# The projection of queries and keys issued ahead of mask and scores on TensorE in 40 slots of a two-branch transformer block

## The chip, the cores and the metric

The kernel runs on one core of one Trainium2 chip. The metric is the device time of one execution in microseconds (us); less is better. All data is float32 (the mask alone is bfloat16).

## The reference

The input x is (4, 1024, 128). After a layer norm two branches read it, and their outputs are added to x: `_L0_attn_ref`, a retention block (16 heads of 8, channel group norms, a small feed-forward part with silu), and `_L0_ffn_ref`, two layers of local attention with a gated feed-forward part. The change lies in the second branch:

```
def _layer(x, wqkv, qs, ksc, wo, lg, lb, w1, b1, w2, b2):
    h = shift_token(x)
    q, k, v = jnp.split(h @ wqkv, 3, axis=-1)      # 8 heads of 64 each
    q = l2norm(q) * qs
    k = l2norm(k) * ksc
    q, k = rotary_xpos(q, k)
    o = local_attention(q, k, v)                   # windows of 64, the own and the one before
    x = x + o @ wo
    h = layernorm(shift_token(x)) * lg + lb
    a, g = jnp.split(h @ w1 + b1, 2, axis=-1)
    return x + (a * gelu(g)) @ w2 + b2
```

## The kernel before

The work goes in steps. A step (l, t) is 128 rows of all four batches in layer l (0 or 1), t from 0 to 7. Every engine runs one list of instructions, written out by hand, in 18 bodies; the engines meet only by semaphores. A body has four slots, k = 0 to 3, one for each batch. In slot k the step `new` projects batch k, the step `old` is finished for batch k, and at slot 0 the step `ff` goes through the feed-forward part. In layer 0 the retention branch of the step follows behind slot 3 (`pe_retention` and its likes on the other engines); in layer 1, for t of 2 and more, slots 1 and 2 hold the small feed-forward part of the retention branch (`block_ffn`).

The attention of one batch is a pipeline over slots. `turned` is the batch projected two slots before: its normalized queries and keys (qkn) are transposed into pT (L1006, then ScalarE copies kT and qT), and its mask (L1025) and scores (L1038) go into pS. `weighted` is the batch projected three slots before: its exponentiated scores pr are transposed into pT (L1049), ScalarE copies them to prT (L540), and they are multiplied with the values into pS (L1064). At the same time batch k of `old` has its output transposed (L1075), copied to oT by ScalarE (L594), multiplied by wo (L1081) and added to the residual by VectorE (xr, L749).

The projection of batch k is two parts on TensorE: the values into bank pV (L1099), and queries and keys into the two banks of pQK (L1133, two matmuls of 128x512). What follows on pQK: ScalarE squares it (sq, L556), VectorE sums the squares (ss, L707), then divides the weighted output (rec and o, L737 and L739), then makes the two products with the rotary tables (m1 and m2, L717, in the rows `m`), each of which adds 1 to `mul_done`. GpSimd makes the norm, the sum and the product qkn from them (L358, L360, L373, L380).

There is one pQK. So L1133 waits until both products of the batch before it are done:

```
need(eng, S["mul_done"], 2 * n)
```

VectorE's order in a slot is: maximum and subtraction of the scores of `turned` (mx L727, pr L729), the residual xr (L749), ss (L707), rec and o, the two products (L717). ScalarE's order is: kT and qT, copies of values and of the shifted input, prT (L540), oT (L594; in slot 0 with a feed-forward part hnT, L545, stands there instead, and then exp, the loading of the gelu table and gelu, L601), sq (L556), exp (L587).

Of the kernel before, what the change touches and what calls it, by code (L numbers as in the profile page):

```python
# [13 lines left out]
NB = 4  # L14
# [72 lines left out]
def need(eng, sem, value):  # L87

    if isinstance(value, int) and value <= 0:
        return  # L90
    eng.wait_ge(sem, value)


def program(nc, a, out):
    with ExitStack() as ctx:
        def sb(name, shape, dt=F32):
            return ctx.enter_context(nc.sbuf_tensor(name, shape, dt))

        def sem(name):
            return ctx.enter_context(nc.semaphore(name))  # L100
# [21 lines left out]
        wqkv = sb("wqkv", [P, DEPTH, 3 * INNER])  # L122
# [35 lines left out]
        hT = sb("hT", [P, NB, P])  # L158
# [54 lines left out]
        pQK = ctx.enter_context(nc.psum_tensor("pQK", [P, 1024], F32))  # L213
# [11 lines left out]
        def score_bank(b):  # L225
# [13 lines left out]
        LS = {n: sem(n) for n in (  # L239
            "carried", "v_kept", "h_ready", "qk_mm", "v_mm", "sq_done", "ss_done", "mul_done", "max_ss", "rn_done", "add_done",  # L240
            "qkn_done", "t_mm", "t_ev", "v_ev", "s_mm", "mx_done", "sub_done", "exp_done",
            "pt_mm", "pt_ev", "o_mm", "rec_done", "o_done", "ot_mm", "ot_ev", "wo_mm", "xr_carried", "xr_done", "hs",
            "ln_mm", "ln_bst", "ln_st", "ln_eps", "ln_rs", "hn_done", "hnt_mm", "hnt_ev", "ag_mm", "gelu_done",
            "hf_done", "w2_mm", "x2_done")}
# [27 lines left out]
        def step_count(step):  # L272

            return NT * step[0] + step[1]

        def count(step, b):
            return NB * step_count(step) + b
# [8 lines left out]
        def at(new, old, k):  # L286

            step = new if k >= 0 else old
            return (step, k % NB, count(step, k % NB)) if step else None
# [708 lines left out]
        def pe_turn(eng, b, n):  # L998

            S = LS  # L1000
            eng.wait_ge(S["qkn_done"], n + 1)
            need(eng, S["t_ev"], 2 * n)
            need(eng, S["pt_ev"], n - 1)
            for half in (1, 0):
                for j in range(4 * half, 4 * half + 4):
                    mm = eng.transpose(pT[:, j * P:(j + 1) * P], qkn[:, b % 2, j * P:(j + 1) * P], ident)  # L1006
                mm.then_inc(S["t_mm"], 1)
# [34 lines left out]
        def pe_turn_weights(eng, b, n, turned):  # L1042
            S = LS
            eng.wait_ge(S["exp_done"], n + 1)
            need(eng, S["pt_ev"], n)
            if turned:
                eng.wait_ge(S["t_ev"], 2 * (n + 2))
            for j in range(8):
                mm = eng.transpose(pT[:, j * P:(j + 1) * P], pr[:, b % 2, j, :], ident)  # L1049
            mm.then_inc(S["pt_mm"], 1)  # L1050
# [18 lines left out]
        def pe_turn_output(eng, n, bank=pM):  # L1069

            S = LS
            eng.wait_ge(S["o_done"], n + 1)
            need(eng, S["xr_done"], n)
            for j in range(4):
                mm = eng.transpose(bank[:, j * P:(j + 1) * P], o[:, j * P:(j + 1) * P], ident)  # L1075
            mm.then_inc(S["ot_mm"], 1)

        def pe_wo(eng, l, n, bank=pM):
            eng.wait_ge(LS["ot_ev"], n + 1)
            for j in range(4):  # L1080
                mm = eng.matmul(bank[:, 0:P], wo[:, l, j, :], oT[:, j, :], start=(j == 0), stop=(j == 3))  # L1081
            mm.then_inc(LS["wo_mm"], 1)

        def pe_slot(eng, new, old, ff, k):
            S = LS
            block_ffn = ff and ff[0] == 1
            turned = at(new, old, k - 2)
            weighted = at(new, old, k - 3)
            if turned:
                pe_turn(eng, turned[1], turned[2])  # L1090
            if k == 0 and old and old[0] == 0:
                pe_retention_out(eng, old[1])
            if new:
                l, n = new[0], count(new, k)
                eng.wait_ge(S["h_ready"], 2 * n + 2)
                need(eng, S["v_ev"], 2 * n)
                if k == 1 and old:
                    eng.wait_ge(S["xr_done"], count(old, 0) + 1)
                eng.matmul(pV[:, :], hT[:, k, :], wqkv[:, l, 1024:1536], start=True, stop=True).then_inc(S["v_mm"], 1)  # L1099
            if k == 1 and block_ffn:  # L1100

                need(eng, S["mul_done"], 2 * n if new else 0)
                eng.wait_ge(G["xa"], 4 * ff[1] + 4)
                for j in range(2):
                    eng.matmul(pQK[:, j * 512:(j + 1) * 512], aT[:, 4 + j, :], xa[:, :, :], start=True,
                               stop=True).then_inc(G["w1_mm"], 1)
            if turned:
                pe_scores(eng, *turned)
            if weighted:
                pe_turn_weights(eng, weighted[1], weighted[2], turned)  # L1110
            if k == 0 and ff:

                ct = step_count(ff)
                eng.wait_ge(S["hn_done"], NB * ct + NB)
                for b in range(NB):
                    mm = eng.transpose(pM[:, b * P:(b + 1) * P], hn[:, b, :], ident)
                mm.then_inc(S["hnt_mm"], 1)
            if k > 0 and old:
                if k == 1 and ff:
                    eng.wait_ge(S["x2_done"], step_count(ff) + 1)  # L1120
                if k == 2 and block_ffn:
                    eng.wait_ge(G["att"], ff[1] + 1)
                if k == 3 and block_ffn:
                    eng.wait_ge(G["osb"], ff[1] + 1)
                pe_turn_output(eng, count(old, k))
            if k == NB - 1 and new and new[0] == 0:
                pe_retention_project(eng, new[1], 0)
            if new:
                need(eng, S["mul_done"], 2 * n)
                if k == 1 and block_ffn:  # L1130
                    eng.wait_ge(G["silu"], 2 * ff[1] + 2)
                for g in range(2):
                    mm = eng.matmul(pQK[:, g * 512:(g + 1) * 512], hT[:, k, :], wqkv[:, l, g * 512:(g + 1) * 512],  # L1133
                                    start=True, stop=True)
                mm.then_inc(S["qk_mm"], 1)
            if k == 0:
                if ff:
                    pe_hidden(eng, ff, (0, 1), turned, weighted)
                if old:
                    if new:  # L1140
                        eng.wait_ge(S["v_ev"], 2 * n + 2)
                    pe_turn_output(eng, count(old, 0), pV)
                if ff:
                    pe_hidden(eng, ff, (2,), turned, weighted)
                    pe_ffn_out(eng, ff, lambda: weighted and pe_values(eng, weighted[1], weighted[2], turned))
            if k > 0 and old:
                pe_wo(eng, old[0], count(old, k))
            if weighted and not (k == 0 and ff):
                pe_values(eng, weighted[1], weighted[2], turned)
            if k == 0 and old:  # L1150
                pe_wo(eng, old[0], count(old, 0), pV)
            if k == 1 and block_ffn:
                eng.wait_ge(G["silu"], 2 * ff[1] + 2)
                eng.wait_ge(S["x2_done"], NT + ff[1] + 1)
                if old:
                    eng.wait_ge(S["xr_done"], count(old, 1) + 1)
                for j in range(2):
                    mm = eng.matmul(pM[:, :], aT[:, 6 + j, :], afh[:, j, :], start=(j == 0), stop=(j == 1))
                mm.then_inc(G["w2_mm"], 1)
            if k == 2 and block_ffn:  # L1160

                eng.wait_ge(G["fin"], ff[1] + 1)
                if old:
                    eng.wait_ge(S["xr_done"], count(old, 2) + 1)
                for b in range(NB):
                    mm = eng.transpose(pM[:, b * P:(b + 1) * P], fin[:, b, :], ident)
                mm.then_inc(G["fin_mm"], 1)
            if k == NB - 1 and old and not (new and new[0] == 0):
                pe_ln(eng, old)
# [130 lines left out]
        def pe_retention_out(eng, t):  # L1300
            eng.wait_ge(A["yt"], t + 1)
            eng.matmul(pS[:, 0:512], aT[:, 3, :], ayT[:, :], start=True, stop=True).then_inc(A["ow_mm"], 1)
# [85 lines left out]
```

## Time and profile before

| What | Value |
|---|---|
| Median of 3 runs | 1004.31 us (1003.1 to 1006.28) |
| Profiled execution | 1006.43 us, of which its span is 1004.6 us |
| TensorE busy | 871.2 us, 87% of the span |
| VectorE busy | 703.5 us, 70% |
| ScalarE busy | 660.7 us, 66% |
| GpSimd busy | 623.5 us, 62% |

The span is what the trace covers, from the first instruction to the last; the time is some 2 us more. A busy share counts an engine's own instructions, and each engine waits for others in between. PE is TensorE (PEld its weight loads), DVE VectorE, ACT ScalarE, POOL GpSimd. A float32 matmul stands in the trace as two records, so the two matmuls of L1133 are "x4".

### The profile page before, as it was taken

The numbers are of one execution on the slowest core, as the hardware profiler recorded it, in microseconds if no ns is written. First come the engines' busy times: TensorE is split into PE (matmuls) and PEld (weight loads), VectorE is DVE, ScalarE is ACT, GpSimd is POOL, SyncE is SP. The second block draws the span as 40 slices with busy tenths as digits, with TensorE's granted clock in tenths as the row PEclk, the third lists the DMA queues.
The fourth block names the chain that finished last, engine by engine and source line by source line (L and its number), as shares of the span: only waits on it lengthen the run. The fifth ranks groups of instructions, "written<-read, shape, count | busy, mean of one in ns | idle before, by whom it ended". The sixth has DMA issues, their size and how long they took to land. (4 is left out here: it accounts for less than half of the span.)

```text
span 1004.6 us, 26321 instructions
## 1 busy us (share of the span) xinstructions
PE 871.2 (87%) x10836; PEld 586.7 (58%) x10836; DVE 703.5 (70%) x1161; ACT 660.7 (66%) x1291; POOL 623.5 (62%) x491
## 2 busy tenths in 40 slices
PE   1677889989899898998989879999999999999876
PEld 1345666766567666676666556565656565656552
DVE  5865766666666667676676766969696969696843
ACT  0444775857758477674785667877786868686633
POOL 4486677675776657666576646757575757575600
PEclk9969999999999899999999989999999999999997
DMA  9100000000000000000000000000000000000000
GB/s 292 21 1 3 1 2 2 2 3 2 2 3 1 3 1 2 3 2 3 2 1 3 2 1 2 1 2 22 2 22 2 22 1 23 2 22 2 22 23 10
DMA packets 20481, 13.47 MB, mean 13 GB/s; under 512 B 4578, under 2 KB 19596, under 8 KB 20236
## 3 DMA queue, kind: packets, MB, share of 16 engines
q1 hardware_dynamic: 15108, 10.49, 3.5%
q10 hardware_dynamic: 5256, 1.31, 0.7%
q8 instruction: 87, 1.43, 0.6%
q14 instruction: 30, 0.25, 0.1%
HBM read 9.70 MB, written 2.10 MB: 12 GB/s over the span
## 5 line engine op out<-in xcount | busy, mean ns | idle before, releaser
L360 POOL TENSOR_TENSOR rn<-rn,half_neg 128x16 f32<-128x16 f32 x64 | 187.6, 2931 | 5.3
L373 POOL TENSOR_TENSOR m<-m 128x1024 f32<-128x1024 f32 x64 | 151.1, 2360 | 0.1
L358 POOL TENSOR_SCALAR rn<-ss 128x16 f32<-128x16 f32 x64 | 16.4, 256 | 199.6 <-DVE ss L707 198.4
L380 POOL TENSOR_TENSOR qkn<-m,rn 128x1024 f32<-128x1024 f32 x64 | 123.8, 1934 | 5.0
L727 DVE TENSOR_REDUCE mx<-pS 128x8 f32<-128x1024 f32 x64 | 78.0, 1219 | 68.7 <-PE pS L1038 68.7
L1133 PE MATMUL pQK<-wqkv,hT 128*128 128x512 f32 x256 | 123.9, 607 | 2.3 <-DVE m L717 2.3
L516 ACT ACTIVATE kT<-pT 128x512 f32<-128x512 f32 x64 | 38.1, 595 | 94.6 <-PE pT L1006 94.1
L556 ACT ACTIVATE sq<-pQK 128x1024 f32<-128x1024 f32 x64 | 65.4, 1022 | 26.4 <-PE pQK L1133 26.3
L707 DVE TENSOR_REDUCE ss<-sq 128x16 f32<-128x1024 f32 x64 | 77.5, 1211 | 6.1 <-ACT sq L556 6.1
L729 DVE TENSOR_TENSOR pr<-pS,mx 128x1024 f32<-128x1024 f32 x64 | 78.4, 1225 | 2.2
L540 ACT ACTIVATE prT<-pT 128x1024 f32<-128x1024 f32 x64 | 65.0, 1016 | 17.4 <-PE pT L1049 16.5
L1064 PEld LDWEIGHTS pS<-vmix,prT 128*64 128x64 f32 x1024 | 64.5, 137 | 20.3 <-issue 15.3
L717 DVE TENSOR_TENSOR m<-pQK,rope 128x1024 f32<-128x1024 f32 x64 | 75.6, 1215 | 0.0
L717 DVE TENSOR_TENSOR m<-pQK,tab 128x1024 f32<-128x1024 f32 x64 | 75.4, 1210 | 0.0
L1006 PE MATMUL pT<-cst,qkn 128*128 128x128 f32 x512 | 70.5, 282 | 5.2 <-POOL qkn L380 4.9
L1064 PE MATMUL pS<-vmix,prT 128*64 128x65 f32 x1024 | 73.2, 225 | 2.1 <-DVE pr L729 2.1
L587 ACT ACTIVATE pr<-pr 128x1024 f32<-128x1024 f32 x64 | 67.6, 1056 | 10.1 <-DVE pr L729 9.1
L1064 PE MATMUL pS<-vown,prT 128*64 128x65 f32 x1024 | 73.3, 225 | 0.0
L1099 PE MATMUL pV<-wqkv,hT 128*128 128x512 f32 x128 | 69.6, 627 | 4.1 <-DVE xr L749 2.1
L1049 PE MATMUL pT<-cst,pr 128*128 128x128 f32 x512 | 69.9, 279 | 0.0
L1192 PE MATMUL pT<-hnT,w 128*128 128x512 f32 (+1 forms) x128 | 62.7, 613 | 6.5 <-DVE hidden L813 5.0
L1038 PE MATMUL pS<-kT,qT 64*64 64x128 f32 x2048 | 68.1, 271 | 0.0
(168 smaller groups left out, 2038.5 us busy)
## 6 DMA issues: line engine op xcount, KB each, us to landing
x<-in_L_attn_x SPq DMA_DIRECT2D x4, 512.0 KB, 9.1
xs<-in_L_attn_x SPq DMA_DIRECT2D x8, 256.0 KB, 2.9
out<-aqkT SPq DMA_DIRECT2D x8, 256.0 KB, 2.2
wqkv<-in_L_ffn_wqkv SPq DMA_DIRECT2D x2, 768.0 KB, 9.9
tab<-in_k_tab SPq DMA_DIRECT2D x1, 1024.0 KB, 10.4
w<-in_L_ffn_w SPq DMA_DIRECT2D x2, 341.0 KB, 10.5
wo<-in_L_ffn_wo SPq DMA_DIRECT2D x2, 256.0 KB
cst<-in_k_cst ACTq DMA_DIRECT2D x1, 404.5 KB, 3.8
```

The lines of the kernel that those rows point to most:

```text
L360: eng.tensor_tensor(rn[:, k % 2, :], rn[:, k % 2, :], half_neg[:, 0:2 * H], ALU.pow).then_inc(S["rn_done"], 1)
L373: eng.tensor_tensor(m1[:, k % 2, :], m1[:, k % 2, :], m2[:, k % 2, :], ALU.add).then_inc(S["add_done"], 1)
L380: eng.tensor_tensor(qkn[:, k % 2, :].rearrange("p (h d) -> p h d", d=DH), m1[:, k % 2, :].rearrange("p (h d) -> p h d", d=DH), rn[:, k % 2 ...
L707: eng.tensor_reduce(ss[:, k % 2, :], sq[:, :].rearrange("p (h d) -> p h d", d=DH), AX.X, ALU.add).then_inc(S["ss_done"], 1)
L717: eng.tensor_tensor(m[:, k % 2, :].rearrange(shape, g=2, h=H, **sizes), src, by, ALU.mult).then_inc(S["mul_done"], 1)
L727: eng.tensor_reduce(mx[:, :], sc, AX.X, ALU.max).then_inc(S["mx_done"], 1)
L729: eng.tensor_tensor(pr[:, b % 2, :, :], sc, mx[:, :].unsqueeze(2).broadcast_to([P, H, P]), ALU.subtract).then_inc(S["sub_done"], 1)
L1006: mm = eng.transpose(pT[:, j * P:(j + 1) * P], qkn[:, b % 2, j * P:(j + 1) * P], ident)
L1049: mm = eng.transpose(pT[:, j * P:(j + 1) * P], pr[:, b % 2, j, :], ident)
L1064: mm = eng.matmul(pS[64 * w:64 * w + 64, col0:col0 + DH + 1], prT[:, i, 64 * w:64 * w + 64], (vown if w else vmix)[b][:, 2 * j + g, :], st ...
L1099: eng.matmul(pV[:, :], hT[:, k, :], wqkv[:, l, 1024:1536], start=True, stop=True).then_inc(S["v_mm"], 1)
L1133: mm = eng.matmul(pQK[:, g * 512:(g + 1) * 512], hT[:, k, :], wqkv[:, l, g * 512:(g + 1) * 512], start=True, stop=True)
```

## The change

In the slots where `new` and `turned` exist, k is 0, 1 or 2, and k = 1 isn't shared with `block_ffn` (which puts its own product into pQK in that slot), the two matmuls into pQK and their wait for `mul_done` are issued directly behind the values' matmul into pV, ahead of mask and scores. In the other slots they stay where they were. No instruction is added or removed. The slots are: slot 2 of step (0,0); slots 0 to 2 of the steps (0,1) to (0,7), (1,0) and (1,1); slots 0 and 2 of (1,2) to (1,7). These are 1 + 27 + 12 = 40 of 64.

```diff
+        def pe_queries_keys(eng, step, k):
+
+            n = count(step, k)
+            need(eng, LS["mul_done"], 2 * n)
+            for g in range(2):
+                mm = eng.matmul(pQK[:, g * 512:(g + 1) * 512], hT[:, k, :], wqkv[:, step[0], g * 512:(g + 1) * 512],
+                                start=True, stop=True)
+            mm.then_inc(LS["qk_mm"], 1)
+
...
                     eng.matmul(pQK[:, j * 512:(j + 1) * 512], aT[:, 4 + j, :], xa[:, :, :], start=True,
                                stop=True).then_inc(G["w1_mm"], 1)
+            early = new and turned and k < NB - 1 and not (k == 1 and block_ffn)
+            if early:
+                pe_queries_keys(eng, new, k)
             if turned:
                 pe_scores(eng, *turned)
...
-            if new:
-                need(eng, S["mul_done"], 2 * n)
+            if new and not early:
                 if k == 1 and block_ffn:
                     eng.wait_ge(G["silu"], 2 * ff[1] + 2)
-                for g in range(2):
-                    mm = eng.matmul(pQK[:, g * 512:(g + 1) * 512], hT[:, k, :], wqkv[:, l, g * 512:(g + 1) * 512],
-                                    start=True, stop=True)
-                mm.then_inc(S["qk_mm"], 1)
+                pe_queries_keys(eng, new, k)
```

The order on TensorE in a slot 1 of layer 0, before:

```order
L1006 MATMUL pT<-cst,qkn 128x128 x8
L1099 MATMUL pV<-wqkv,hT 128x512
L1025 MATMUL pS<-mask 64x512 x4
L1038 MATMUL pS<-kT,qT 64x128 x16
L1049 MATMUL pT<-cst,pr 128x128 x8
L1075 MATMUL pM<-cst,o 128x128 x4
L1133 MATMUL pQK<-wqkv,hT 128x512 x2
L1081 MATMUL pM<-oT,wo 128x128 x4
```

and with the change:

```order
L1006 MATMUL pT<-cst,qkn 128x128 x8
L1108 MATMUL pV<-wqkv,hT 128x512
L1089 MATMUL pQK<-wqkv,hT 128x512 x2
L1025 MATMUL pS<-mask 64x512 x4
L1038 MATMUL pS<-kT,qT 64x128 x16
L1049 MATMUL pT<-cst,pr 128x128 x8
L1075 MATMUL pM<-cst,o 128x128 x4
L1081 MATMUL pM<-oT,wo 128x128 x4
```

The pair into pQK has moved ahead of mask, scores and both transposes, and the product with wo now follows the transposes directly. Line numbers behind the new function are 8 or 9 higher.

The order on TensorE in slot 0 of a step of layer 0 with a feed-forward part, before:

```order
L1099 MATMUL pV<-wqkv,hT 128x512
L1025 MATMUL pS<-mask 64x512 x4
L1038 MATMUL pS<-kT,qT 64x128 x16
L1049 MATMUL pT<-cst,pr 128x128 x8
L1116 MATMUL pM<-cst,hn 128x128 x4
L1133 MATMUL pQK<-wqkv,hT 128x512 x2
L1192 MATMUL pT<-hnT,w 128x512 x2
```

and with the change:

```order
L1108 MATMUL pV<-wqkv,hT 128x512
L1089 MATMUL pQK<-wqkv,hT 128x512 x2
L1025 MATMUL pS<-mask 64x512 x4
L1038 MATMUL pS<-kT,qT 64x128 x16
L1049 MATMUL pT<-cst,pr 128x128 x8
L1128 MATMUL pM<-cst,hn 128x128 x4
L1200 MATMUL pT<-hnT,w 128x512 x2
```

Here the pair stood between the transposes of hn and the first matmul on hnT; now nothing does. The lists of VectorE, ScalarE, GpSimd and the queues are the same as before.

## Rows read from the trace of the kernel before

**Rows 1.** The page, shares of the span in the chain that ended last.

```profile
PE 20%; DVE 18%; ACT 7%; issue 3%; POOLq 0%; POOL 0%; DVEq 0%; ACTq 0%
```

**Rows 2.** The page, costliest groups: busy, mean ns, idle before, releaser.

```profile
L727 DVE TENSOR_REDUCE mx<-pS 128x8 f32<-128x1024 f32 x64 | 78.0, 1219 | 68.7 <-PE pS L1038 68.7
```

**Rows 3.** Timeline, slot 1 of (0,4): start us, duration us, engine, line.

```profile
302.76 1.02 PE L1099 MATMUL pV<-wqkv,hT 128*128 128x512 f32 x2
303.71 0.41 PE L1025 MATMUL pS<-mask 64*64 64x512 bf16 x4
304.93 1.09 PE L1049 MATMUL pT<-cst,pr 128*128 128x128 f32 x8
305.08 1.23 DVE L727 TENSOR_REDUCE mx<-pS 128x8 f32<-128x1024 f32 x1 [2.64 <-PE pS L1038]
...
306.23 1.01 ACT L540 ACTIVATE prT<-pT 128x1024 f32<-128x1024 f32 x1
306.30 1.88 PE L1133 MATMUL pQK<-wqkv,hT 128*128 128x512 f32 x4
...
307.13 0.59 ACT L594 ACTIVATE oT<-pM 128x512 f32<-128x512 f32 x1
308.01 1.05 PE L1081 MATMUL pM<-oT,wo 128*128 128x128 f32 x8
308.21 1.02 ACT L556 ACTIVATE sq<-pQK 128x1024 f32<-128x1024 f32 x1 [0.49 <-PE pQK L1133]
309.11 0.29 DVE L749 TENSOR_TENSOR xr<-pM,xnT 128x128 f32<-128x128 f32 x1 [1.54 <-PE pM L1081]
...
309.31 1.21 DVE L707 TENSOR_REDUCE ss<-sq 128x16 f32<-128x1024 f32 x1
...
311.28 2.35 DVE L717 TENSOR_TENSOR m<-pQK,rope 128x1024 f32<-128x1024 f32 x2
```

**Rows 4.** Timeline, slot 2 of the same step.

```profile
311.01 1.02 PE L1099 MATMUL pV<-wqkv,hT 128*128 128x512 f32 x2
...
311.96 0.41 PE L1025 MATMUL pS<-mask 64*64 64x512 bf16 x4
```

**Rows 5.** Timeline, slot 0 of the next step of layer 0.

```profile
349.84 1.02 PE L1099 MATMUL pV<-wqkv,hT 128*128 128x512 f32 x2
...
350.94 0.41 PE L1025 MATMUL pS<-mask 64*64 64x512 bf16 x4
...
355.23 1.88 PE L1192 MATMUL pT<-hnT,w 128*128 128x512 f32 x4
```

**Rows 6.** Timeline, slot 0 of a step of layer 1.

```profile
689.40 2.32 DVE L717 TENSOR_TENSOR m<-pQK,tab 128x1024 f32<-128x1024 f32 x2
...
690.25 0.41 PE L1025 MATMUL pS<-mask 64*64 64x512 bf16 x4
...
692.91 1.21 DVE L727 TENSOR_REDUCE mx<-pS 128x8 f32<-128x1024 f32 x1
```

**Rows 7.** Timeline, slot 2 of a step of layer 1.

```profile
668.89 2.35 DVE L717 TENSOR_TENSOR m<-pQK,tab 128x1024 f32<-128x1024 f32 x2
...
672.55 1.09 PE L1049 MATMUL pT<-cst,pr 128*128 128x128 f32 x8
...
674.30 1.21 DVE L727 TENSOR_REDUCE mx<-pS 128x8 f32<-128x1024 f32 x1
```

**Rows 8.** The chain that ended last, in the same slot: start, us, what.

```profile
677.02 1.15 PE pS L1064 x32
```

**Rows 9.** Timeline of two idle times of TensorE, in brackets.

```profile
112.04 1.10 PE L1099 MATMUL pV<-wqkv,hT 128*128 128x512 f32 x2 [2.13 <-DVE xr L749]
...
333.87 0.69 PE L1227 MATMUL pM<-cst,aqk 128*128 128x128 f32 x2 [3.14 <-DVE aqk L830]
```

**Rows 10.** Windows: busy (x) by engine, and the granted clock behind POOL's.

```profile
302.00:310.20 8.20, 8.20 (x104) 6.05 (x103) 3.84 (x5) 7.06 (x12) 1.72 (x1) 1.00 0.00 0
...
318.40:349.00 30.60, 26.07 (x580) 20.49 (x580) 20.43 (x43) 17.20 (x56) 20.99 (x24) 0.89 0.01 3
```

**Rows 11.** Line L1133: duration ns min/median/max.

```profile
L1133 PE MATMUL pQK<-wqkv,hT x256: 592/592/1221, 43.4 to 934.3; 128*128 128x512 f32 x128
```

## The prediction

> **What bounds the kernel now.** I read the chain that ended last first: it runs through all engines, with TensorE 20% and VectorE 18% of the span named [rows 1]. So no engine is the bound by itself; the slots are a loop of waits. The groups with their waits say where it is tight: VectorE waits 68.7 us in all for the scores, ahead of mx [rows 2]. Then the timeline, slot by slot. A slot 1 of layer 0 lasts 8.25 us (from the values' matmul at 302.76 to the next at 311.01) [rows 3, 4], and TensorE is busy for 8.20 of 8.20 us in it [rows 10]. Its list is full, and every engine's list runs in order. What a new order on TensorE is worth is therefore read from who waits for each piece: mx waited 2.64 us for the scores, xr waited 1.54 us for the product with wo, and sq waited only 0.49 us for pQK [rows 3]. The change brings forward the piece that was waited for least, and puts it ahead of the two that were waited for most.
>
> **The change, part by part.** Nothing is added. One instruction pair and its wait move, so there are two prices: the time of the pair ahead of the scores, and the wait that now holds everything behind it.
>
> The pair takes TensorE from 306.30 to the next start at 308.01, that is 1.71 us; one such matmul is half, 0.86 us [rows 3]. A signal from one engine to the next costs about 0.05 us (the product with wo ends at 309.06, xr starts at 309.11) [rows 3].
>
> *Slot 1 (no wait).* The products of slot 0 are long over. The values' matmul leaves TensorE free at 302.76 + 0.86 = 303.62, and the pair ends at 305.33; mask and scores start there, not at 303.71, so 1.62 late. The transposes of the weights come from 304.93 to 306.55 and end, with their 1.09, at 307.64. ScalarE's list is unchanged: prT, then oT, then sq. prT runs 307.69 to 308.70 (it was at 306.23), oT starts 0.1 before that ends, 308.60 to 309.19, and the product with wo starts at 309.24 in place of 308.01 [rows 3]. The cover is gone: the pair used to run on TensorE while ScalarE made prT and oT. Now TensorE has nothing there and stands still for about a microsecond. pQK is ready at 305.5, some 3.6 us before sq can start behind oT, so its earliness buys nothing. sq starts at about 309.1 in place of 308.21, xr and ss are bound by the product with wo and come 1.2 late [rows 3]. So do m, and TensorE's next slot. Slot 1 costs 1.2 us.
>
> *Slot 2 of layer 0 (the wait bites).* Before, VectorE's two products of slot 1 ran from 311.28 to 313.63 [rows 3] while TensorE already made the scores from 311.96 [rows 4]. Now the pair needs them over, and mask, scores and both transposes are queued behind it; VectorE in turn needs those scores next. Shifted by 1.2, the values' matmul ends at 313.1 and the products at 314.85. TensorE stands still for 1.8 us, the pair runs 314.9 to 316.6, and mask and scores start at 316.6 in place of 311.96: 4.6 late. From mask to the product with wo the way was 4.30 us (303.71 to 308.01) and is 309.24 - 305.33 = 3.9 without the pair in it. So the product with wo comes 4.6 - 4.3 + 3.9 = 4.2 late, and with it xr, ss and m. Slots 1 and 2 together cost 4.2 us. What follows (slot 3, the retention part) is a chain on the same engines, and I carry all of it on.
>
> *Slot 0 of layer 0.* No wait, since the products of the last batch lie before the retention part. TensorE is free at 349.84 + 0.86 = 350.70, mask starts at 352.41 in place of 350.94 [rows 5]: 1.5 late. The transposes of the weights, prT, hnT, exp, the table load and gelu follow one another on ScalarE, so the 1.5 stays in it. The pair's old place before the first hidden matmul (355.23) [rows 5] falls empty, as ScalarE's hnT isn't ready any sooner. Price 1.5 us.
>
> *Slot 0 of layer 1, from step (1,1).* The products of slot 3 end at 691.72 while mask started at 690.25. The pair now runs 691.77 to 693.48, mask follows, and mx, 1.37 behind the start of the mask (303.71 to 305.08) [rows 3], comes at 694.85 in place of 692.91 [rows 6]. Price 1.9 us; pr, exp and gelu hang on it.
>
> *Slot 2 of layer 1, from (1,2).* The products end at 671.24, just when TensorE comes to the pair, so 1.7 late for mask and transposes. mx is not hurt: it was at 674.30 behind other work of VectorE [rows 7] and would be possible at 674.4. The transposes end at 672.55 + 1.7 + 1.09 = 675.3; prT and oT as above lead to a product with wo at 676.9, and the weighted values' product (L1064), some 0.9 behind that start (its 1.05 less the run-out), at 677.8 in place of 677.02 [rows 8]. Price 0.8 us.
>
> *Sum.* Eight steps, (0,1) to (0,7) and (1,0), at 1.5 + 4.2 = 5.7: 45.6. Step (1,1) at 1.9 + 4.2: 6.1. Six steps (1,2) to (1,7) at 1.9 + 0.8: 16.2. Slot 2 of (0,0) stands in the slow start and I take it as nothing (at most one 4.2). Total 68 us on a span of 1004.6, so 1072.5. The profiled execution (1006.4) lies 2.1 above the median; against the median of 1004.3 the forecast is 1072.
>
> **Bounds of what the trace doesn't show.** How much of a delay later slack eats: at the least only the stalls count, 1.8 in nine slots 2 and 1.7 in seven slots 0, 28 us; at the most nothing is eaten and each of the 40 slots pays the whole 1.7 beside the stalls, 28 + 68 = 96. I take 68, near the middle, since the slots were followed to the next slot's start. A gain is not excluded for pieces I didn't follow: VectorE's xa (L880) may run beside less GpSimd work when it comes later.
>
> **The rivals.**
> *Faster.* The pair fills a gap that TensorE has ahead of the mask, where it waits for ScalarE's qT, and the product with wo is then free to go at oT. In favour: xr waits 1.54 us for that product. The mechanism decides where the gap is 1.7 us or more. The rows show 303.71 - 303.62 = 0.09 in slot 1, 0.09 in slot 2 and 0.24 in slot 0 [rows 3 to 5]. Were the pair free there, the product with wo could start at oT's end, 307.77 in place of 308.01, and 40 slots would give 10 us: 994. I give it 0.03.
> *No change.* VectorE's wait for the scores takes the delay in and something else sets the end. Against it: that wait is on VectorE and grows with the delay, and TensorE's own list ran 8.20 of 8.20 us. 1004, chance 0.02.
> *Half of it eaten.* Only the stalls count: 1004 + 28 = 1032, anything from 1015 to 1050. Chance 0.1.
> *The clock falls.* TensorE now stands still twice in a slot, for 1.8 and 1.0 us. The retention part, with an idle time of 3.14 us in it, had a granted clock of 0.89 where slot 1 had 1.00; after an idle time of 2.13 us the values' matmul took 1.10 against 1.02, so nothing fell [rows 3, 9, 10]. The largest single wait I expect is 1.8 us, below that one. At the 1.2 GHz level a record of the pair takes up to 1221 ns against 592 [rows 11]; the pair, scores and transposes (4 us at 2.4 GHz) would last up to 4 us more, in the sixteen slots with a stall up to 64 us: 1136. Some of it in some of the slots is likelier, 1100 and up; chance 0.08.
> The Trainium skill (TensorE: Matmul & The Clock Gate, the section on HAM oscillation) has the same mechanism, waits between bursts of matmuls that bring the slower clock back. By that rule the two idle times here would end nearer to 1136 than to 1072 if they counted together; the trace agrees with it on the long wait of the retention part alone.
>
> **How the numbers follow.** My own case has 0.77 and its own range is 1050 to 1100: the sum of 68, down to 46 if a third is eaten, up to 96 if nothing is. The half-eaten case, the falling clock and the two small ones hold the other 0.23, so this is also the range of 8 in 10. A measurement of this kernel tells 0.3% (3 us) from no change. Slower by more than that: 0.77 + 0.1 + 0.08 = 0.95. Same 0.02, faster 0.03.
>
> **What the changed profile would show.** In a slot 2 of layer 0 an idle time of TensorE ahead of the pair (L1089) released by VectorE's m, about 1.8 us, some sixteen such waits in all; the slot from values' matmul to values' matmul longer by about 3 us (11.3); a new wait of about 1 us of TensorE for oT ahead of L1081 in the moved slots; sq no longer waiting for pQK there; VectorE's wait for the scores well above 68.7 us; steps of layer 0 longer by 5.7 us, and those of layer 1 from (1,2) on by 2.7. Wrong would be: sq starting earlier than before relative to the slot, or TensorE finding `mul_done` already given in slot 2, which would need VectorE's products earlier than the rows allow. The forecast would also fail if VectorE, freed of something, caught up in slot 3 or in the retention part.

## The result, and the profile after

| | Median | Runs | Ratio to before |
|---|---|---|---|
| before | 1005.29 us | 1003.1 to 1006.28 (4) | |
| with the change | 1087.9 us | 1084.93 to 1090.18 (4) | 1.0797 (95%: 1.0765 to 1.0829) |

The row before has one run more than the table ahead of the prediction. The change makes the kernel 8% slower, 82.6 us. The profiled execution has a span of 1088.2 us, 83.6 more than before. The page of the changed kernel, busy shares and the chain that ended last by engine, the latter beside [rows 1]:

```profile
PE 891.2 (82%) x10836; PEld 589.7 (54%) x10836; DVE 694.2 (64%) x1161; ACT 660.4 (61%) x1291; POOL 622.5 (57%) x491
...
PE 27%; ACT 10%; DVE 7%; issue 4%; POOLq 0%; POOL 0%; ACTq 0%; DVEq 0%
```

TensorE's instructions are the same 10836 as before, and their records 20 us longer (its mean granted clock is 0.963 in place of 0.970, and the first record behind a wait is 0.1 us longer, of which more below); the other engines' work is the same or less. What has grown is the waiting. In the chain ScalarE has risen from 7% to 10% and VectorE has fallen from 18% to 7%: the way now leads over ScalarE's copies. The waits, of TensorE and of VectorE (engine, line, waited for, us in total, times, longest); the row of mx answers to [rows 2]:

```profile
PE pM L1081 <- ACT oT L594: 34.9, 33, 1.2
PE pQK L1089 <- DVE m L717: 30.1, 18, 3.7
...
PE pT L1200 <- ACT hnT L545: 17.7, 16, 1.2
```

```profile
DVE mx L727 <- PE pS L1038: 144.7, 56, 5.0
```

The same three waits of TensorE in the kernel before:

```profile
PE pM L1081 <- ACT oT L594: 7.0, 9, 1.2
...
PE pQK L1133 <- DVE m L717: 2.3, 2, 1.3
...
PE pT L1192 <- ACT hnT L545: 1.4, 2, 0.7
```

Before, TensorE waited 7.0 us for oT and 2.3 us for m at these places. Now it waits 34.9 us for oT, 30.1 us for m and 17.7 us for hnT (1.4 before): about 72 us of new idle time on the engine whose list was full. VectorE's wait for the scores has doubled from 68.7 to 144.7 us.

The timeline of slots 1 and 2 of (0,4), the slots of [rows 3] and [rows 4], 24 us later in the span:

```profile
326.71 1.02 PE L1108 MATMUL pV<-wqkv,hT 128*128 128x512 f32 x2
...
327.57 1.88 PE L1089 MATMUL pQK<-wqkv,hT 128*128 128x512 f32 x4
...
329.38 0.41 PE L1025 MATMUL pS<-mask 64*64 64x512 bf16 x4
...
330.60 1.09 PE L1049 MATMUL pT<-cst,pr 128*128 128x128 f32 x8
330.74 1.23 DVE L727 TENSOR_REDUCE mx<-pS 128x8 f32<-128x1024 f32 x1 [4.36 <-PE pS L1038]
...
331.73 1.02 ACT L540 ACTIVATE prT<-pT 128x1024 f32<-128x1024 f32 x1 [1.45 <-PE pT L1049]
...
332.65 0.59 ACT L594 ACTIVATE oT<-pM 128x512 f32<-128x512 f32 x1
...
333.13 1.03 ACT L556 ACTIVATE sq<-pQK 128x1024 f32<-128x1024 f32 x1
...
333.29 1.16 PE L1081 MATMUL pM<-oT,wo 128*128 128x128 f32 x8 [1.16 <-ACT oT L594]
...
334.49 0.29 DVE L749 TENSOR_TENSOR xr<-pM,xnT 128x128 f32<-128x128 f32 x1 [1.26 <-PE pM L1081]
...
336.39 1.02 PE L1108 MATMUL pV<-wqkv,hT 128*128 128x512 f32 x2
...
336.66 2.35 DVE L717 TENSOR_TENSOR m<-pQK,rope 128x1024 f32<-128x1024 f32 x2
...
339.06 1.98 PE L1089 MATMUL pQK<-wqkv,hT 128*128 128x512 f32 x4 [1.65 <-DVE m L717]
...
340.98 0.41 PE L1025 MATMUL pS<-mask 64*64 64x512 bf16 x4
```

Both prices of the prediction stand in it. In slot 1 the pair is finished at 329.45, but sq, which reads it, starts at 333.13: the early pQK lies unused for 3.7 us. TensorE then has nothing between the output transposes and the product with wo and stands still for 1.16 us, until oT is there. In slot 2 the pair waits for the products of slot 1 (336.66 to 339.01), 1.65 us in which the mask could have run.

The starts of the values' matmul (L1099, now L1108) divide the trace into slots. A slot's length is the distance to the next start; this table is worked out from both traces, and from the traces of the experiments below:

```
extra length against before, us     predicted   change   range over its steps
slot 0, layer 0 and (1,0)              1.5        1.57     1.57 to 1.58
slot 1, same steps and (1,1)           1.2        1.43     1.42 to 1.44
slot 2, same steps and (1,1)           3.0        3.34     3.33 to 3.35
slot 0, (1,1)                          1.9        2.15
slot 0, (1,2) to (1,6)                 1.9        1.92     1.91 to 1.93
slot 0, (1,7)                          1.9        3.56     (lower clock)
slot 2, (1,2) to (1,7)                 0.8        1.17     1.09 to 1.19
slots 1 of (1,2) on, 3 of (1,1)-(1,6)  0          0.00     -0.01 to 0.01
the whole of step (0,0)                0          3.90
slot 3 with retention, (0,1) to (0,7)  0         -0.12 in all (-1.61 to 1.30 each)
```

The moved slots of one kind repeat to about 0.01 us (slot 2 of (1,6) was 0.09 longer than its like before, which gives the 1.09), so most of the result can be read from one trace. Step (0,0), slot 3 with the retention part and slot 3 of (1,0) scatter: (1,0)'s is 1.0 longer here, and 1.1 longer in e7 below, where the pair stays in its old place.

### The profile page after: what moved, and what is told of

Same layout as the page of the kernel before. It is cut to its first block and busy times, and to the rows that moved or that the text cites. A ratio compares the mean times of both kernels' runs of the same rounds, so it can differ in the third digit from the quotient of the medians.

```text
span 1088.2 us, 26321 instructions
## 1 busy us (share of the span) xinstructions
PE 891.2 (82%) x10836; PEld 589.7 (54%) x10836; DVE 694.2 (64%) x1161; ACT 660.4 (61%) x1291; POOL 622.5 (57%) x491
## 3 DMA queue, kind: packets, MB, share of 16 engines
q8 instruction: 87, 1.43, 0.6%
## 5 line engine op out<-in xcount | busy, mean ns | idle before, releaser
L727 DVE TENSOR_REDUCE mx<-pS 128x8 f32<-128x1024 f32 x64 | 78.3, 1223 | 144.7 <-PE pS L1038 144.7
L1089 PE MATMUL pQK<-wqkv,hT 128*128 128x512 f32 x256 | 129.0, 628 | 30.1 <-DVE m L717 30.1
L1089 PEld LDWEIGHTS pQK<-wqkv,hT 128*128 128x128 f32 x256 | 47.5, 198 | 94.5 <-DVE m L717 50.0
L1081 PE MATMUL pM<-oT,wo 128*128 128x128 f32 x384 | 54.0, 284 | 34.9 <-ACT oT L594 34.9
L1200 PE MATMUL pT<-hnT,w 128*128 128x512 f32 (+1 forms) x128 | 65.2, 634 | 17.7 <-ACT hnT L545 17.7
L1081 PEld LDWEIGHTS pM<-oT,wo 128*128 128x128 f32 x384 | 47.7, 191 | 53.5 <-ACT oT L594 48.5
L1108 PE MATMUL pV<-wqkv,hT 128*128 128x512 f32 x128 | 69.1, 623 | 2.6 <-ACT hT L495 1.4
```

The lines of the kernel that those rows point to most:

```text
L727: eng.tensor_reduce(mx[:, :], sc, AX.X, ALU.max).then_inc(S["mx_done"], 1)
```

## The experiments

Each is compared with the kernel before, run on the same chip. The slots are those of one trace of each kernel.

**e1, the wait alone.** The order of before; in the 40 slots the wait is put ahead of the mask:

```diff
+            early = new and turned and k < NB - 1 and not (k == 1 and block_ffn)
+            if early:
+                need(eng, S["mul_done"], 2 * n)
             if turned:
                 pe_scores(eng, *turned)
```

> The order of before, but in the 40 slots TensorE waits for both products of the batch before (mul_done) ahead of the mask, as the change does; the pair into pQK stays behind the transposes. Theory A (two prices: the wait ahead of the scores, and ScalarE's copies left without cover): only the wait is paid. In nine slots 2 (layer 0, (1,0), (1,1)) mask starts at 313.68 in place of 311.96, 1.7 us each, 15 us; in the seven stalled slots 0 of layer 1 mx comes only 0.3 us late and the hidden part 1 us, 0.3 to 1 each, 2 to 7 us; the other slots nothing. Sum 18 to 22, about 1024 us. Theory B (the wait is all of it): near the changed kernel, 1088. Theory C (the order is all of it): 1005.

1024.94 us (1020.62 to 1026.68) against 1006.19: ratio 1.0169 (1.0119 to 1.0219), 18.8 us. Theories B and C fall, A gives the size. The mask in slot 2 of (0,4), whose values' matmul starts at 316.89:

```profile
319.56 0.41 PE L1025 MATMUL pS<-mask 64*64 64x512 bf16 x4 [1.64 <-DVE m L717]
```

The slots: 1.71 in each of the nine slots 2 of layer 0, (1,0) and (1,1) (expected 1.7), 0.10 in slot 1, 0.24 in slot 0 of (1,1), and 0.01 at most in slot 0 of (1,2) on, where I had allowed 0.3 to 1. So in layer 1 the wait costs little by itself; it only costs with the pair's 1.7 us behind it. (The 0.23 between (1,1) and the later steps stands in e2 and in the change as well; it is VectorE's xa, which (1,1) doesn't have, as the last section shows.)

**e2, the pair behind the scores.** In the 40 slots mask and scores go first, then the pair with its wait, then the transposes of the weights:

```diff
-            if early:
-                pe_queries_keys(eng, new, k)
             if turned:
                 pe_scores(eng, *turned)
+            if early:
+                pe_queries_keys(eng, new, k)
             if weighted:
                 pe_turn_weights(eng, weighted[1], weighted[2], turned)
```

> In the 40 slots the pair into pQK with its wait stands behind mask and scores, ahead of the transposes of the weights. Theory A (the binding way is transposes of the weights, prT, oT, product with wo): slots 0 and 1 of layer 0 cost as in the changed kernel, 1.6 and 1.4 us, though mx is not late; slot 2 of layer 0 2.0 in place of 3.3; slot 0 of layer 1 1.0 in place of 1.9; slot 2 of layer 1 1.2 as before. Sum 8 x 5.0 + 4.4 + 6 x 2.2 = 57, about 1062 us. Theory D (the price is VectorE getting its scores late): with the scores back in time nearly all is given back, 1005 to 1015.

1060.86 us (1058.93 to 1061.55), ratio 1.0528 (1.0483 to 1.0572). Theory D, that the late scores of VectorE are nearly all of the price, falls. Slot 1 of the same step shows it:

```profile
319.93 1.02 PE L1108 MATMUL pV<-wqkv,hT 128*128 128x512 f32 x2
...
322.10 1.98 PE L1089 MATMUL pQK<-wqkv,hT 128*128 128x512 f32 x4
...
322.25 1.23 DVE L727 TENSOR_REDUCE mx<-pS 128x8 f32<-128x1024 f32 x1 [2.64 <-PE pS L1038]
...
324.99 1.02 ACT L540 ACTIVATE prT<-pT 128x1024 f32<-128x1024 f32 x1 [1.50 <-PE pT L1049]
...
325.91 0.59 ACT L594 ACTIVATE oT<-pM 128x512 f32<-128x512 f32 x1
...
326.56 1.16 PE L1081 MATMUL pM<-oT,wo 128*128 128x128 f32 x8 [1.17 <-ACT oT L594]
```

mx comes 2.32 us behind the values' matmul and waits 2.64, exactly as before the change [rows 3], and still the slot is 1.48 us longer (the change: 1.43): the transposes of the weights are late, so are prT and oT, and TensorE waits 1.17 us for oT. The slots otherwise: slot 0 of layer 0 1.77, slot 2 1.98 (expected 2.0), in layer 1 from (1,2) on 0.56 (expected 1.0) and 1.08. A part of the price does go away with the scores in front: 1.36 us in each slot 2 of layer 0 (3.34 to 1.98) and as much in slot 0 of (1,1) on (1.92 to 0.56), that is, in the sixteen slots with a stall, where TensorE now makes the scores while it would have waited.

**e3, only the slots without a stall.** The pair is moved in 17 slots:

```diff
             early = new and turned and k < NB - 1 and not (k == 1 and block_ffn)
+            early = early and (k == 1 or (k == 0 and new[1] <= (7 if new[0] == 0 else 0)))
```

> The pair is moved in only the 17 slots where both products of the batch before are long over: slots 0 and 1 of (0,1) to (0,7) and (1,0), slot 1 of (1,1). Theory A: 8 x (1.57 + 1.43) + 1.4 = 25 us, about 1030 us. Theory B (the wait is all of it): 1005.

1033.21 us (1029.21 to 1034.78), ratio 1.0246 (1.0198 to 1.0294), 27 us where 25 were expected. The moved slots are 1.58 and 1.43 longer (slot 1 of (0,1) 3.07, of which more below), the slots 2 behind them 0.00. TensorE's waits in this kernel:

```profile
PE pM L1081 <- ACT oT L594: 17.5, 18, 1.2
...
PE pQK L1089 <- DVE m L717: 2.4, 2, 1.4
```

It waits for m at the pair for 2.4 us in two places, as the kernel before did (2.3 in two), and 17.5 us for oT in place of 7.0. So the order by itself costs this much, without the wait.

**e4, the square first.** ScalarE reads the early pQK early, in the moved slots 1 and 2:

```diff
+            if square_first:
+                eng.wait_ge(S["qk_mm"], n + 1)
+                need(eng, S["ss_done"], n)
+                eng.activation(sq[:, :], pQK[:, :], ACT.Square).then_inc(S["sq_done"], 1)
             if weighted:
                 eng.wait_ge(S["pt_mm"], weighted[2] + 1)
```

> The changed kernel, and in its moved slots 1 and 2 ScalarE's square of pQK goes ahead of prT and oT, so that the early pQK is used early. Theory A (what binds is transposes, prT, oT, product with wo; ss stands behind xr on VectorE anyway): nothing is won, 1085 to 1089 us. Theory E (the move fails only because sq is queued behind prT and oT): sq comes 2 to 3 us sooner, and the 0.9 us that it was late in 25 slots is won, 1065 us or less.

1092.54 us (1081.39 to 1096.92), ratio 1.0864 (1.0814 to 1.0913). Nothing is won; theory E falls. The times scatter more than expected (a span of 1079.6 in the profiled execution), but the moved slots 1 and 2 don't: 1.43 and 3.34, as in the change. Of the 8.6 us by which this span is below the change's, 4.9 are in the retention parts, 1.6 in slot 0 of (1,7) and 1.2 in step (0,0), none of them where the edit is. Slot 1 of (0,4):

```profile
327.28 1.01 ACT L542 ACTIVATE sq<-pQK 128x1024 f32<-128x1024 f32 x1
...
330.39 1.16 PE L1086 MATMUL pM<-oT,wo 128*128 128x128 f32 x8 [1.17 <-ACT oT L599]
...
331.80 1.21 DVE L712 TENSOR_REDUCE ss<-sq 128x16 f32<-128x1024 f32 x1
```

sq is made 3.5 us ahead of ss, and ss starts as late as ever, behind xr, which is behind the product with wo, which waits for oT.

**e5, the pair one place later still,** behind the transposes of the weights and ahead of the output transposes (the edit of e2, one block further down).

> In the 40 slots the pair with its wait stands one place later still: behind the transposes of the weights, ahead of the output transposes (in slot 0: ahead of those of hn). Theory A: scores and prT are as in the kernel before and the products of VectorE are over when TensorE gets to the pair, so no stall; only oT (or hnT) comes late. Slots 1 and 2 of layer 0: output transposes end at 308.2, product with wo at 308.9 in place of 308.0, 0.95 us each; slot 0 of layer 0 1.45 us through hnT and exp; layer 1 from (1,2) 0.25 and 0.8. Sum 8 x 3.35 + 2.2 + 6 x 1.05 = 35, about 1040 us: between 1005 and the 1061 of the place behind the scores. A theory in which any move ahead of the transposes costs the same 1.7 us of TensorE gives 1060.

1034.87 us (1030.06 to 1038.91) against 1007.73: ratio 1.0262 (1.021 to 1.0314); expected 1040. Slots 1 and 2 of layer 0 are 0.96 and 0.95 longer (expected 0.95), slot 0 1.25 (1.45), layer 1 0.00 and 0.55 (0.25 and 0.8); slot 1 of (0,1) stands out with 2.58. The price falls with each piece that goes back ahead of the pair.

**e6, the output transposes first, in the changed kernel.** In slots 1 and 2 both TensorE and ScalarE make the output's transposition ahead of the weights':

```diff
+            if k in (1, 2) and old:
...
+                pe_turn_output(eng, count(old, k))
             if weighted:
                 pe_turn_weights(eng, weighted[1], weighted[2], turned)
...
+            if k in (1, 2):
+                act_output(eng, old, k)
             if weighted:
                 eng.wait_ge(S["pt_mm"], weighted[2] + 1)
```

(The waits that belong to the output transposes move with them, and their old places keep slot 3 alone.)

> The changed kernel, and in slots 1 and 2 the output transposes (L1075) go ahead of the transposes of the weights on TensorE and oT ahead of prT on ScalarE, so that oT is made while TensorE transposes the weights. Theory A (TensorE stands still for oT at the product with wo because nothing covers ScalarE's two copies): that wait of some 1.2 us goes; of it about 0.5 is won a slot by VectorE's way and 1.0 by TensorE's. Slots 1 and 2 of layer 0 together 3.3 in place of 4.8 us, slot 2 of layer 1 0.3 in place of 1.2: some 19 us less than the changed kernel, about 1068. If the order of TensorE alone mattered and not the copies' cover: 1088.

1076.69 us (1071.75 to 1078.75), ratio 1.0677 (1.0624 to 1.073); expected some 1068. The wait for oT is gone. Slot 1 of (0,4):

```profile
330.19 0.60 ACT L596 ACTIVATE oT<-pM 128x512 f32<-128x512 f32 x1 [1.01 <-PE pM L1077]
...
330.86 1.14 PE L1083 MATMUL pM<-oT,wo 128*128 128x128 f32 x8
...
333.03 1.22 DVE L709 TENSOR_REDUCE ss<-sq 128x16 f32<-128x1024 f32 x1 [0.71 <-ACT sq L558]
```

Slot 1 costs 0.54 in place of 1.43 (what is left shows at ss, which now waits 0.71 us for sq, made behind the late prT), slot 2 of layer 1 0.69 in place of 1.17 (and slot 1 of (1,2) to (1,7), not a moved one, is 0.91 shorter), and five of the nine slots 2 cost 2.8 to 2.95 in place of 3.34, as theory A has it. But four of the nine, (0,1), (0,6), (0,7) and (1,0), cost 4.4 to 4.8; these and slot 2 of layer 1 (0.69 where 0.3 was expected) are what the expectation missed. Slot 2 of (0,6), and the windows of it and of (0,5) (us, busy by engine, granted clock behind POOL's):

```profile
472.51 1.02 PE L1110 MATMUL pV<-wqkv,hT 128*128 128x512 f32 x2
...
475.52 2.89 PE L1091 MATMUL pQK<-wqkv,hT 128*128 128x512 f32 x4 [1.99 <-DVE m L719]
...
478.34 0.64 PE L1027 MATMUL pS<-mask 64*64 64x512 bf16 x4
...
478.77 1.58 PE L1040 MATMUL pS<-kT,qT 64*64 64x128 f32 x32
```

```profile
472.50:485.00 12.50, 10.12 (x103) 6.65 (x102) 6.78 (x8) 7.20 (x13) 7.35 (x4) 0.86 0.00 1
403.00:415.00 12.00, 9.44 (x104) 6.07 (x102) 7.89 (x10) 8.34 (x17) 8.33 (x5) 1.00 0.00 0
```

The pair takes 2.89 us in place of 1.98 in (0,5), and the scores 1.58 in place of 1.04: part of the stretch is at the 1.2 GHz level, after a wait of 1.99 us. The five slots 2 that kept the clock had the same wait ahead of the pair, 1.99 to 2.00 us. The slot is 1.64 us longer by it (12.68 against 11.04).

**e8, the stall filled.** e6, and in the nine slots 2 TensorE works through the wait:

```diff
             if early:
+                if k == 2 and old and not block_ffn:
+                    need(eng, S["xr_done"], count(old, k))
+                    for _ in range(12):
+                        eng.transpose(pM[:, 3 * P:4 * P], ident, ident)
                 pe_queries_keys(eng, new, k)
```

> The kernel with the pair early and the output transposes first (the one that measured 1076.7 us), and in nine slots 2 (layer 0 and the first two steps of layer 1) twelve transposes of the identity matrix into an unused quarter of pM (L1093 or near) stand ahead of the pair's wait, so that TensorE works through the stall instead of standing still. They add work that nobody reads and leave the computation as it is. In the profile of the kernel without them, four of these slots took 4.4 to 4.8 us more than before and the others 2.8, with the pair at the lower clock in the long ones. Theory F (the clock falls when TensorE stands still in the stall): all nine stay at 2.8 (up to 0.3 more, where the last of the twelve ends behind the products); 1065 to 1075 us. Theory G (the long slots have another cause): three or four slots are again at 4.4, 1077 us.

1068.57 us (1064.71 to 1075.79) against 1006.35: ratio 1.0643 (1.0598 to 1.0687). The twelve transposes and the pair behind them, slot 2 of (0,6):

```profile
467.36 1.47 PE L1123 MATMUL pM<-cst 128*128 128x128 f32 x12
...
469.51 1.98 PE L1091 MATMUL pQK<-wqkv,hT 128*128 128x512 f32 x4 [0.68 <-DVE m L719]
```

All nine slots 2 cost 2.8 (3.04 in (1,0)). Extra work has made these slots no longer, and the four long ones are gone. That is what theory F expects, in one trace of each kernel. It is not proof: in the traces of the change and of e4 the same nine slots, with a stall of 1.65 us and nothing in it, kept the clock too. The medians of e6 and e8 come from different chips and their ranges overlap, so they don't settle it either.

**e7 and e9, the swap of e6 in the kernel before,** in all slots 1 and 2 (e7), and in slot 1 of (1,2) to (1,7) alone (e9).

> The same swap in the kernel before. Theory A: there the pair covers ScalarE's copies already in slots 1 and 2 of layer 0, so nothing is won there; in slot 1 of layer 1, where ScalarE is late (the product with wo waits 0.7 us for oT), sq and ss come 0.3 us sooner, at most 2 us in all. 1002 to 1006 us. If the copies' order were worth something by itself: 995 or less.

> The kernel before with the output transposes and oT first in slot 1 of the steps (1,2) to (1,7) alone. Theory A: slot 1 is 0.91 us shorter as with the swap in all slots, and slot 2, which ends by VectorE's list, gives 0.5 of it back, with or without a swap of its own; so 0.4 us a step, 2.5 us in all, 1002 to 1005 beside 1005 to 1008. If the 0.5 in slot 2 was the price of the swap in slot 2, slot 2 is as before and the whole is 5.5 us.

e7: 1003.13 us (1000.7 to 1008.2) against 1007.73, ratio 0.9973 (0.9948 to 0.9998). e9: 1003.01 us (997.25 to 1006.26) against 1006.35, ratio 0.9965 (0.9945 to 0.9985). Slots 1 and 2 of layer 0 are 0.00 different in e7: where the pair stands in its old place it covers ScalarE's copies, and their order is worth nothing. Slot 1 of layer 1 is 0.91 shorter in both, and slot 2 gives 0.3 to 0.5 of it back in both, so the giving back is not the price of the swap in slot 2. What is left is 6 x 0.5 = 3 us. Both are about 0.3% faster than the kernel before, with intervals that just leave out 1, and can't be told from each other: the pair where it was, and in that one slot the copy that TensorE waits for first.

## Why the prediction was right, and where it was short

*Direction and mechanism.* Right. 68 us were forecast and 82.6 measured, within 1050 to 1100 and within the likeliest case. The step "the cover is gone" is shown by e3 (no stall, 1.58 and 1.43 us a slot), by e2 (scores on time, same price in slot 1) and from the other side by e6 (copies swapped, the wait for oT gone). The step "the wait bites" is shown by e1: 1.71 in each slot 2. Together they nearly add up, 1.43 + 1.71 = 3.14 of the 3.34.

*"pQK is ready ... its earliness buys nothing."* Right in the trace of the change and, for slots 1 and 2, shown by e4: even read at once it buys nothing.

*"Slot 1 costs 1.2 us."* It cost 1.43, and two terms were 0.1 short. The mask followed the values' matmul by 0.95 us and now follows it by 2.67, so 1.72 late and not 1.62: I took the 0.09 us between the values' matmul and the mask for a wait into which the pair would fit, and it is still there behind the pair. And the product with wo takes 1.16 in place of 1.05: before, its first weight load started 0.24 us ahead of the first matmul, under the pair; now load and matmul both start at 333.29, and the first record lasts 377 ns in place of 273. Slot 0 of layer 0 has the first term alone (1.57 for 1.5). Slot 2 (3.34 for 3.0) and slot 2 of layer 1 (1.17 for 0.8) have both, and a third of the same kind: the pair itself, now behind a wait, takes 1.98 in place of 1.88. Over the moved slots such tenths are most of 8 us of the shortfall.

*"Slot 0 of layer 1 ... Price 1.9 us."* The number came out, 1.92, but partly by luck. mx came 2.14 late and not 1.9 (760.85 - 754.89 = 5.96 behind the values' matmul, where it was 3.82), and slot 0 of (1,1) is 2.15 longer. From (1,2) to (1,6) VectorE's xa is shorter than before and gives 0.23 back, which the prediction named as possible and didn't count; the rows are in the last section.

*"Slot 2 of (0,0) ... I take it as nothing (at most one 4.2)."* The nothing was wrong, by 3.9 us in this trace and by 1.7 to 2.7 in those of e4, e6 and e8, which have the same early pair there. It failed by leaving the place out: the products that the pair waits for end late, and the clock falls.

```profile
62.14 3.68 PE L1089 MATMUL pQK<-wqkv,hT 128*128 128x512 f32 x4 [3.74 <-DVE m L717]
```

TensorE waits 3.74 us there (1.05 before) and the pair then takes 3.68 us in place of 1.98.

*"The clock falls"*, the rival with 0.08. It did in (0,0) above, and in one of the sixteen stalled slots that the rival spoke of, slot 0 of (1,7), 3.56 in place of 1.92:

```profile
969.90 3.54 PE L1089 MATMUL pQK<-wqkv,hT 128*128 128x512 f32 x4 [1.55 <-DVE m L717]
```

So it was not a case of its own but a small part of mine: 1.64 us once, some of (0,0)'s 3.9, and in e6 four slots 2 and slot 0 of (1,7) again. My argument against it, that the single wait of 1.8 us is below one of 2.13 that did no harm [rows 9], was not sound: here the clock was low behind a wait of 1.55 us, and in five other steps the same wait of the same slot left it high (1.98 us for the pair in (1,3)). Nor was the row of 2.13 us good evidence: in e3 the same wait, 2.12 us, stands ahead of the same values' matmul in slot 1 of (0,1), and the pair that now follows it took 3.25 us:

```profile
113.78 1.10 PE L1108 MATMUL pV<-wqkv,hT 128*128 128x512 f32 x2 [2.12 <-DVE xr L749]
114.71 3.25 PE L1089 MATMUL pQK<-wqkv,hT 128*128 128x512 f32 x4
```

The fall came a microsecond behind the wait, where only the matmuls that follow show it. It is the 1.64 us by which that slot of e3 exceeds the others. In e5 the same matmul behind the same wait was itself slow:

```profile
110.34 1.75 PE L1108 MATMUL pV<-wqkv,hT 128*128 128x512 f32 x2 [2.13 <-DVE xr L749]
```

*The rest of the 15 us.* Worked out from the slots: moved slots 77.9 for 68, of which 1.64 is clock; step (0,0) 3.9; slot 3 of (1,0) 1.0; the rest below 1. The retention parts sum to -0.1, as forecast ("I carry all of it on"), but that it came out so near is luck: in the traces of e1 to e9 the same seven slots lie between 5.1 us below and 6.1 us above those of the kernel before. Much of this goes with the clock. Slot 3 of (0,2), the whole slot, before and with the change (columns as in [rows 10]):

```profile
191.77:222.27 30.50, 25.26 (x574) 19.28 (x573) 20.47 (x43) 17.03 (x56) 21.97 (x23) 0.94 0.01 2
```

```profile
209.91:238.80 28.89, 23.68 (x574) 18.24 (x573) 20.29 (x43) 16.42 (x54) 21.89 (x23) 1.00 0.01 3
```

In the eleven traces this slot takes 28.5 to 28.9 us in the five where the granted clock stays at 1.00 in it, and 30.2 to 31.3 in the six where it doesn't. Why the clock falls in the one trace and not in the other stays open.

*The other rivals.* "Faster" rested on a gap ahead of the mask, and there is none: in slot 1 the mask follows directly behind the pair. "No change" and "half of it eaten": slots 1 and 3 of layer 1, behind the moved ones, gave nothing back (0.00); of the retention parts the scatter leaves only the time as a whole, which is 1088 and not 1032.

## What to carry to other kernels

Before a piece of work is moved forward on an engine with a full list, look at what it lies beside: here 1.7 us of matmuls covered two copies on ScalarE, and the piece that was waited for least (0.49 us) went ahead of those waited for most. A result that comes early is worth nothing if its reader is queued behind something that the move has made late; e4 and e2 are the cheap ways to ask which it is, one by reading early, the other by moving in half steps. And what a wait costs depends on what is queued right behind it: in slot 0 of (1,1) it cost 0.24 us ahead of the mask alone (e1), and 2.15 with the 1.7 us pair between it and the mask.

## What the runs showed of the hardware

The clock of TensorE did not follow the length of the wait just ahead: 1.55 us of waiting was followed by the 1.2 GHz level in one step and by the 2.4 GHz level in five others with the same slot, to 0.02 us. In e6 nine waits of 1.99 to 2.00 us in the same slot were followed by the lower level four times and by the higher one five times. With that wait filled by transposes that nobody reads (e8) none of the nine slots fell. The Trainium skill (TensorE: Matmul & The Clock Gate, the section on HAM oscillation) names waits between bursts of matmuls as what brings the slower clock back. The direction agrees with e6; but the waits of its example are longer ones, for transfers, and it doesn't tell why a wait of 1.55 or 1.99 us is followed by the lower level in some of these slots and not in others.

VectorE's four operations xa (L880) have a median of 340 ns and a maximum of 2058 ns, in the kernel before. They took 3.89 us in slot 0 of (1,3) before (1395, 2057, 333 and 334 ns) and 1.97 us with the change (1204, then 335 to 338 ns), where they started later against GpSimd's products:

```profile
694.25 2.36 POOL L373 TENSOR_TENSOR m<-m 128x1024 f32<-128x1024 f32 x1
...
695.30 3.89 DVE L880 TENSOR_SCALAR xa<-x,gsc,gsh 128x128 f32<-128x128 f32 x4
...
696.69 1.90 POOL L380 TENSOR_TENSOR qkn<-m,rn 128x1024 f32<-128x1024 f32 x1
```

```profile
762.47 1.90 POOL L380 TENSOR_TENSOR qkn<-m,rn 128x1024 f32<-128x1024 f32 x1
...
763.25 1.97 DVE L880 TENSOR_SCALAR xa<-x,gsc,gsh 128x128 f32<-128x128 f32 x4
```

Each of the long ones ends just behind a product of GpSimd: the first two before at 696.69 and 698.67, behind products that end at 696.61 and 698.59, the first with the change at 764.45, behind 764.37. The ones that start behind the last product take about 335 ns, and so do all four in slot 0 of (1,7) with the change (336 to 344 ns), where they start 0.5 us behind it. That an operation of VectorE was held until GpSimd's was over is what the rows suggest; no run here separates it.

The later start shortened xa by 1.9 us in that slot, but only 0.23 of it reached the slot. Before, the operation behind xa (hidden, L813, which multiplies by gelu's result) started without a wait behind xa, so that ss came 10.67 us into the slot, 0.25 later than in (1,1), where there is no xa and hidden waits for gelu. With the change hidden waits 1.33 us for ScalarE's gelu and ss for sq, so the way through gelu, 2.15 later than before, sets the end: 2.15 less 0.23 is the 1.92.
